# Record vectors of a recurrence block moved by DMA instead of turned on VectorE, in a decoder layer on Trainium2

## What is computed

```python
def step(S, inp):
    qt, kt, vt, at, gft = inp
    bs1 = jnp.einsum('bhk,bhkv->bhv', kt, S)
    S1 = S + at[..., :, None] * bs1[..., None, :]
    S2 = jnp.exp(gft)[..., None] * S1
    bs2 = jnp.einsum('bhk,bhkv->bhv', kt, S2)
    S3 = S2 + at[..., :, None] * bs2[..., None, :] + kt[..., :, None] * vt[..., None, :]
    o = jnp.einsum('bhk,bhkv->bhv', qt, S3)
    return (S3, o)
out = out3[:, -N:]   # out3 stacks z, z, o: only the last third of the steps' outputs are used
```

## Time and profile before

| | us |
|---|---|
| median of 3 runs | 2278.86 |
| lowest, highest | 2270.1, 2287.62 |
| the profiled execution | 2289.55 |
| its span | 2287.8 |
| DVE busy | 1961.8 (86%) |
| PE busy | 1758.8 (77%) |
| POOL busy | 1179.1 (52%) |
| ACT busy | 688.7 (30%) |

### The profile page before, as it was taken

How to read it: one execution, slowest core, us unless ns; L and a number is a source line. 1 busy time by engine, 2 the same in 40 slices (tenths; PEclk the granted TensorE clock), 3 DMA queues, 4 the chain that set the end, 5 groups by cost and what they waited for, 6 DMA issues and landing times.

```text
span 2287.8 us, 34138 instructions
## 1 busy us (share of the span) xinstructions
PE 1758.8 (77%) x10406; PEld 1336.9 (58%) x10406; DVE 1961.8 (86%) x5667; ACT 688.7 (30%) x1377; POOL 1179.1 (52%) x1477
## 2 busy tenths in 40 slices
PE   6278988998898889988998440268888799877993
PEld 3145767676667666776677320145675567755682
DVE  7999998999999999999899998999999999733000
ACT  3132244323432343234323100162223622243120
POOL 2445364564565545655575479474775665223103
PEclk8568998999999989998999765577998689977997
DMA  7111443354434444543355321110364133620353
GB/s 251 61 29 60 141 142 101 129 161 146 142 126 134 146 112 136 154 146 111 116 173 168 83 97 32 30 20 14 107 191 153 20 101 129 220 80 24 108 189 104
DMA packets 319121, 262.29 MB, mean 115 GB/s; under 512 B 157297, under 2 KB 292074, under 8 KB 318954
## 3 DMA queue, kind: packets, MB, share of 16 engines
q1 hardware_dynamic: 284874, 218.08, 30.8%
q10 hardware_dynamic: 27936, 25.44, 3.4%
q0 software_dynamic: 6144, 16.79, 2.3%
HBM read 217.82 MB, written 41.03 MB: 113 GB/s over the span
## 4 chain that ended last, share of the span: by engine, by line
PE 39%; DVE 33%; POOL 9%; ACT 7%; issue 6%; DMA 4%; SPq 2%; ACTq 0%; POOLq 0%; DVEq 0%; PEldq 0%
PE ps L740 9%; PE ps L731 8%; DVE ps L1750 7%; DVE ps L1731 6%; PE ps L676 5%; PE ps L667 5%; DVE prod L1723 5%; DVE terms L1738 4%; DVE terms L1733 3%; PE ps L613 2%; PE ps L600 2%; PE ps L624 1%; ACT hT L1054 1%; DMA pj<-in_wpT 1%; DVE rec_out L1672 1%
## 5 line engine op out<-in xcount | busy, mean ns | idle before, releaser
L1750 DVE TENSOR_REDUCE ps<-terms 128x64 f32<-128x320 f32 x1024 | 448.6, 483 | 0.0
L1731 DVE TENSOR_REDUCE ps<-prod 128x16 f32<-128x272 f32 x1024 | 397.2, 433 | 0.0
L1738 DVE TENSOR_TENSOR terms<-ps,rec_out 128x256 f32<-128x256 f32 x1024 | 381.8, 414 | 0.0
L731 PE MATMUL ps<-xg,fc 128*128 128x128 f32 x2848 | 356.5, 286 | 32.9 <-PE ps L740 11.5
L1723 DVE TENSOR_TENSOR prod<-ps,rec_in 128x256 f32<-128x256 f32 x1024 | 380.7, 413 | 0.1
L731 PEld LDWEIGHTS ps<-xg,fc 128*128 128x128 f32 x2848 | 346.1, 201 | 54.6 <-issue 46.9
L740 PE MATMUL ps<-pj,hT 128*128 128x256 f32 x1424 | 334.3, 388 | 32.8 <-ACT hT L1054 32.8
L740 PEld LDWEIGHTS ps<-pj,hT 128*128 128x128 f32 x1424 | 265.9, 192 | 85.7 <-ACT hT L1054 52.3
L667 PE MATMUL ps<-xtf,fc 128*128 128x512 f32 x512 | 244.6, 616 | 5.7 <-issue 3.4
L676 PE MATMUL ps<-pj,hT 128*128 128x256 f32 x1024 | 236.5, 382 | 0.0
L676 PEld LDWEIGHTS ps<-pj,hT 128*128 128x128 f32 x1024 | 195.1, 191 | 57.1 <-issue 34.4
(11 more groups left out here) (257 smaller groups left out, 3003.7 us busy)
## 6 DMA issues: line engine op xcount, KB each, us to landing
fc<-in_wfcT SPq DMA_DIRECT2D x80, 1024.0 KB, 5.1
pj<-in_wpT SPq DMA_DIRECT2D x80, 1024.0 KB, 7.9
xg_rows<-in_rows ACTq DMA_DIRECT2D x105, 128.0 KB, 2.1
rec_in<-early_rows SPq DMA_DIRECT2D x60, 192.0 KB, 2.8
out_rows<-y ACTq DMA_DIRECT2D x89, 128.0 KB, 5.7
early_rows<-vec SPq DMA_DIRECT2D x180, 32.0 KB
in_rows<-o_rows SPq DMA_DIRECT2D x2, 2176.0 KB, 17.5
out_rows<-o_rows SPq DMA_DIRECT2D x2, 2176.0 KB, 18.1
```

The lines of the kernel that those rows point to most:

```text
L731: i = mm(ps[:, UP + g // 4, g % 4 * P:(g % 4 + 1) * P], fc[:, par, c, g * P:(g + 1) * P], xg[:, c], start=c == 0, stop=c == KC - 1)
L1731: red(SE[:, old, cols, HD:EH].rearrange("p v n -> p n v"), prod[:, c % PLACED, :, cols, 0:HD + 1], AX.X, ALU.add).then_inc(step_done, 1)
L1738: tt(terms[:, cols, :, 0:NV], SE[:, old, cols, HD:EH].unsqueeze(2).to_broadcast([P, HC, HD, NV]), rec_out[:, c].unsqueeze(1).to_broadcast( ...
L1750: red(SE[:, new, cols, 0:HD], terms[:, cols, :, 0:NV + 1], AX.X, ALU.add).then_inc(step_done, 1)
```

## The change

- `vec` loses the slots of w and k. They move to `wk_rows`, with the four words of a vector element (two steps, w and k) side by side, so that one run of 64 words per chunk and head is what `rec_out` holds. `wk` is a view of it with a step of four words; ACT writes k into it (one more activation a step), POOL reads and writes it.
- From block 1 on, `lay_out` turns nothing but the queries of kept blocks. DVE waits for the end of POOL's list only in kept blocks. It waits for `early_in0` and `late_in0` ahead of a block's first chunk, and for `early_in1` and `late_in1` ahead of chunk 16's values.
- The values go with the early moves: 8 more DMAs to DRAM, each of 1,024 runs of 32 bytes, and one more read per half. They come first, behind `kv_sb` alone.
- `late_vectors` waits for operation 42 (47 for a kept block), writes w, k (4 DMAs, runs of 256 bytes) and the last input vector (4 DMAs, 64 bytes), waits for them to land and issues `late_records`, 4 reads per half. The list has the last product on `E_COL` ahead of those on z.
- `LAY` goes: POOL and ACT no longer wait for DVE's transposes of these vectors; ACT waits for `late_out`.
- POOL's list of a free block ends at chunk 27 instead of 32.
- In `FREE_AT` and `LATER_AT` steps are placed 1 to 5 later.

```diff
-LAY = CH + NV + 1
-LAY_KEPT = LAY + 2 * CH
+LAY_KEPT = 2 * CH
+LATE_READY, LATE_READY_KEPT = 42, 47
+        wk_rows = sb("wk_rows", [P, D, CH, 2])
+        wk = wk_rows[:, :, :, :].rearrange("p d i c -> p c i d")
...
             def early_vectors(sb_at):
+                sp.wait_ge(kv_sb, (sb_at + 1) * CH)
+                for b in range(B):
+                    rows = slice(b * NCH, (b + 1) * NCH)
+                    for i in range(CH):
+                        sp.dma_start(early_vals[rows].rearrange("g (n i v) -> n i g v", n=NCH, i=CH)[:, i],
+                                     vec[rows, i, V_COL].rearrange("n (g v) -> n g v", v=HV)).then_inc(early_out, 16)
                 sp.wait_ge(prep_pool, prep_before(sb_at) + EARLY_READY)
...
+            def late_vectors(sb_at):
+                if sb_at > 1:
+                    sp.wait_ge(late_in1, (sb_at - 1) * (LATE_READS * 16))
+                sp.wait_ge(prep_pool, prep_before(sb_at) + (LATE_READY_KEPT if sb_at >= KEEP else LATE_READY))
+                for b in range(B):
+                    rows = slice(b * NCH, (b + 1) * NCH)
+                    sp.dma_start(late_wk[b].rearrange("h (n x) -> n h x", n=NCH),
+                                 wk_rows[rows].rearrange("n d i c -> n (d i c)").rearrange("n (h x) -> n h x", h=H)).then_inc(late_out, 16)
+                    sp.dma_start(early_rows[EARLY, b].rearrange("h (n d) -> n h d", n=NCH),
+                                 vec[rows, 1, E_COL].rearrange("n (h d) -> n h d", h=H)).then_inc(late_out, 16)
+                sp.wait_ge(late_out, sb_at * (LATE_MOVES * 16))
+                late_records(sb_at, 0, late_in0)
...
+            def second_half(sb_at):
+                early_records(sb_at, 1, early_in1)
+                late_records(sb_at, 1, late_in1)
...
                 used(f, LATE + 1)
                 if m is not None:
                     early_vectors(first)
+                    late_vectors(first)
                 used(f, LATE + 2)
...
-                early_records(first, 1, early_in1)
+                second_half(first)
...
                 used(m, 0)
                 early_vectors(first + 1)
+                late_vectors(first + 1)
                 if f is not None:
                     store_tile(f)
                 for e in EXPERTS[1:3]:
                     used(m, e)
-                early_records(first + 1, 1, early_in1)
+                second_half(first + 1)
...
-                last = PREP_DONE_LATE if late else PREP_DONE_KEPT if keep else NCH
+                last = PREP_DONE_LATE if late else PREP_DONE_KEPT if keep else PREP_DONE
...
-                dve.wait_ge(prep_pool, prep_before(sb_at + 1))
-                for i in range(CH):
-                    nc.vector.transpose(vrec[:, :, i].rearrange("p n v -> p v n"), ...)
+                if sb_at == 0 or kept:
+                    dve.wait_ge(prep_pool, prep_before(sb_at + 1))
...
-                across(rec_in[:, NV - 1], by_d(vec[:, 1, E_COL]))
-                for i in range(CH):
-                    for kind in range(2):
-                        across(rec_out[:, :, :, 2 * i + kind], by_d(vec[:, i, (W_COL, K_COL)[kind]]))
...
+                if sb_at:
+                    dve.wait_ge(early_in0, sb_at * (EARLY_READS * 16))
+                    dve.wait_ge(late_in0, sb_at * (LATE_READS * 16))
                 place_v(0)
...
-FREE_AT = {1: 1, "caps": 46, "minima": (40, 42, 43, 44), "divided": 61, "resid": 66, 2: 66, "routing": 85, "places": 93, "rows": 94, "gather": 82, "scatter": 95, "combine": 101, 3: 112}
+FREE_AT = {1: 1, "caps": 46, "minima": (41, 43, 44, 45), "divided": 64, "resid": 70, 2: 70, "routing": 90, "places": 98, "rows": 99, "gather": 84, "scatter": 100, "combine": 103, 3: 114}
```

More of the change, by code:

```diff
@@ L73 @@
 PREP_FROM, PREP_FROM_KEPT, PREP_FROM_SECOND, PREP_DONE_KEPT = 13, 5, 4, 29
-PREP_FROM_LATE, PREP_DONE_LATE = 10, 31
+PREP_FROM_LATE, PREP_DONE_LATE, PREP_DONE = 10, 31, 27
 LAY_FIRST = CH + 2 * NV + 1
-LAY = CH + NV + 1
-LAY_KEPT = LAY + 2 * CH
-KC_SLOTS = W_COL, K_COL, V_COL, XK_COL, E_COL = range(5)
+LAY_KEPT = 2 * CH
+W_COL, K_COL = range(2)
+V_COL, XK_COL, E_COL = range(3)
 EARLY = NV
 EARLY_READY = 26
-EARLY_MOVES = EARLY * B
+VALUE_MOVES = CH * B
+EARLY_MOVES = EARLY * B + VALUE_MOVES
+EARLY_READS = 5
+LATE_READY, LATE_READY_KEPT = 42, 47
+LATE_MOVES = 2 * B
+LATE_READS = 4
 HALF = NCH // 2
@@ L348, in early_records @@
                 chunks = slice(half * HALF, (half + 1) * HALF)
+                sp.dma_start(vrec[:, chunks].rearrange("g n i v -> g (n i v)"),
+                             early_vals[:, half * (HALF * CH * HV):(half + 1) * (HALF * CH * HV)]).then_inc(done, 16)
                 for dst, kind in ((rec_in[:, 0:EARLY - 1, chunks], slice(0, EARLY - 1)), (rec_g[:, chunks].unsqueeze(1), slice(EARLY - 1, EARLY))):
@@ L352, in early_records, with late_records @@
                         sp.dma_start(dst[v:P:2].rearrange("q c n d -> q c (n d)"), src).then_inc(done, 16)
+            def late_vectors(sb_at):
[10 more added lines that the diff above has]
+                late_records(sb_at, 0, late_in0)
+            def late_records(sb_at, half, done):
+                sp.wait_ge(step_done, (sb_at - 1) * (NCH * STEP) + 2 + (half + 1) * (HALF * STEP))
+                chunks = slice(half * HALF, (half + 1) * HALF)
+                for dst, src in ((rec_out[:, chunks].rearrange("q n d k -> q (n d k)"), late_wk.rearrange("b h n -> (b h) n")),
+                                 (rec_in[:, NV - 1, chunks].rearrange("q n d -> q (n d)"), early_rows[EARLY].rearrange("b h n -> (b h) n"))):
+                    n = src.shape[1] // 2
+                    for v in range(2):
+                        sp.dma_start(dst[v:P:2], src[:, half * n:(half + 1) * n]).then_inc(done, 16)
+            def second_half(sb_at):
+                early_records(sb_at, 1, early_in1)
+                late_records(sb_at, 1, late_in1)
             def store_tile(m):
@@ L1653, in first_preparation @@
                 then(tt(heads(e), heads(zp[:, :]), by_head(hsum[:, 3]), ALU.mult))
-                for kind, col in enumerate((K_COL, E_COL)):
+                for kind, col in enumerate((wk[:, K_COL, 1], vec[:, 1, E_COL])):
                     after()
-                    then(tt(zp[:, :], z, by_step(vec[:, 1, col]), ALU.mult))
+                    then(tt(zp[:, :], z, by_step(col), ALU.mult))
                     sums(dots[:, kind])
```

66 lines of the change are left out of this document (37 added, 29 removed).

## The result

The changed kernel takes 2374.7 us (median of 4, 2366.45 to 2382.3), the kernel before 2275.71 in the same comparison (2270.1 to 2287.62): ratio 1.0414, 95% interval 1.038 to 1.0448. It is 4.1% slower. I had predicted 2248, and the result lies above my whole range.

The account below looks back on a forecast made before the run. VectorE was taken as the bound, PE next. Terms summed to -31.2 us, taken as -31: 2289.55 profiled to 2258.5, or 2248 against the 2278.86 median; own range 2237 to 2257, 8 in 10: 2222 to 2283.

Parts of the forecast that it names:

- 19.6 us of waits that PE would get back: In periods 1 to 4: 15.6 us for shifted scores, 1.5 for `chosen`, 2.5 for an expert's weights.
- DVE bounds, PE some 8 us behind: In period 2 VectorE is busy 223.7 of 224.9 us; with its load gone PE is the next bound.
- PE gets back the scores' wait, -15.6: In periods 1 to 4, earlier minima on VectorE end PE's wait for shifted scores: 4 x 3.9 us.
- Rival 2: PE gives nothing back, as the scores' wait is a chain only partly VectorE's: 2263 us, chance 0.18.
- the two smaller waits: PE's waits in period 2 for `chosen` (1.46 us) and an expert's weights (2.46 us), both counted as regained.
- Late rows priced at 0: At boundaries in periods 1 to 4, VectorE's waiting for PE covers the late rows; bound 2 us at each of five boundaries.
- Value moves at 0.53 us each: In the SP queue, each of 8 more DMAs per block takes 0.53 us to issue, hidden behind the wait for GpSimd.
- Rival 4: Value moves of 32-byte runs drain slowly, 8 taking 17 us instead of 4: about +60 us, 2308, chance 0.12.
- POOL's strides at 0: GpSimd's operations on keys and w 4 words apart cost nothing extra, judged from 32-element tree additions.
- Rival 3: GpSimd slows by its strides, half as much again on some 15 operations per block: +28 to +31, about 2278, chance 0.12.
- Later steps, +1.8 and -7.5: Five steps' later routing starts period 0 1.8 us late; behind tile 4's routing, five steps fewer gain 7.5 us.
- From tile 4's routing to the end, -18.8: VectorE leads again: -7.5 for fewer steps, -5.7, -5.7 and -3.1 at boundaries, +3.2 for the output store behind five reads.

Follow-up runs that it names:

- b2_list27: The kernel before with only GpSimd's list in a free block ended at chunk 27 instead of 32: ratio 0.9966.
- d2_strides: The changed kernel with all rows turned by VectorE and steps at the old places, leaving interleaved rows and the list to chunk 27: 1.0115, 2305.8 us.
- d1_all_dve: As d2_strides, but with the steps at the later places of the changed kernel: 1.0259, 2342.8 us.
- a4_values_dve: The changed kernel with the values turned by VectorE again and no value moves or reads by DMA: 1.0216, 2333.9 us.
- a1_divided: The changed kernel with "divided" at step 62, ahead of the block boundary, instead of 64: 1.0271, 2350.6 us.
- a3_values_apart: The changed kernel with the eight value moves issued one load earlier in the SP queue: 1.0248, 2341.1 us.
- d4_filler7: d1_all_dve with 7 idle matmuls of 128 rows ahead of PE's wait for "divided": 1.0169, 2318.1 us.
- c2_mix: The changed kernel with values turned by VectorE, second weights load ahead of late rows, "divided" at 62 and list to chunk 30: 1.0091, 2302.7 us.

## Why the prediction was wrong

Set one behind the other, the runs make a ledger from the kernel before to the changed one. Each ratio is known to 0.3 or 0.5%, so the first line to 7 us, and each other one, a difference of two ratios, to some 15.

| added | runs compared | us |
|---|---|---|
| list to chunk 27 | b2_list27, before | -8 |
| w and k four words apart (with one more activation a step and the list's new order) | d2_strides, b2_list27 | +34 |
| steps placed later | d1_all_dve, d2_strides | +33 |
| w, k, last row by DMA | a4_values_dve, d1_all_dve | -10 |
| values by DMA | changed kernel, a4_values_dve | +45 |
| together | | +94 |

The steps that failed are terms of the sum: 0 for the value moves, 0 for the strides, nothing for the first preparation, and later steps as a gain of 5.7 us on balance. Above all the sum counted 19.6 us of waits that PE would get back. By the steps of the prediction:

- **DVE bounds, PE some 8 us behind.** Right as far as it was tested: filling PE's stop on b2_list27 gave nothing, and DVE's busy time fell by 65 us. How far behind PE is, no run measures by itself.
- **PE gets back the scores' wait, -15.6.** Wrong. It is 3.88 us in periods 1 to 4 of every run in which no filler stands ahead of it. Rival 2 had the number, but not the reason, and nor had I: neither DVE nor POOL is in this wait. Here it is in period 2, before and then after (ACT, and POOL's shift of the same scores):

```profile
571.20 2.25 POOL L1234 TENSOR_TENSOR probs<-probs,least 128x1232 f32<-128x1232 f32 x1 [3.49 <-DVE least L1484]
574.33 0.39 ACT L1060 ACTIVATE y<-ps 128x256 f32<-128x256 f32 x1 [3.62 <-PE ps L740]
575.42 1.28 ACT L964 ACT_TABLE_LOAD   x1 [0.70 <-ACT y L1060]
576.71 2.36 ACT L964 ACTIVATE probs<-probs 128x1232 f32<-128x1232 f32 x2
...
600.29 4.46 POOL L1289 TENSOR_TENSOR probs<-probs,least 128x1232 f32<-128x1232 f32 x2
602.50 0.38 ACT L1115 ACTIVATE y<-ps 128x256 f32<-128x256 f32 x1 [3.62 <-PE ps L793]
603.59 1.28 ACT L1019 ACT_TABLE_LOAD   x1 [0.70 <-ACT y L1115]
604.88 2.35 ACT L1019 ACTIVATE probs<-probs 128x1232 f32<-128x1232 f32 x2
```

  Before, the first shift is done at 573.45, ahead of ACT. What ACT does is copy out PE's own last pass, load a table and take the first exponential, 3.88 us from PE's last matmul whatever the others do. Even the later shift of the changed kernel (two in the row, the first done near 602.5) is there in time. No earlier DVE could have given this back. With 64 us of DVE work taken off (a4_values_dve against d1_all_dve), the gain is 10 us, not told from none. Of the two smaller waits the 1.46 us for `chosen` did go in period 2; the 2.46 for weights became 7.5 to 8.3 at the ends of periods 1 to 3.
- **Late rows priced at 0.** Wrong. I let DVE's wait for PE at "resid", step 70, cover the rows' way. But rows are wanted at the boundary, step 64, and behind it, ahead of "resid", stands "divided", which PE waits for. DVE may have time left at step 70; PE has lost its own by then. What I called a bound of 0 to 2 us is 4.4 to 11.4 us at 10 boundaries, 71.4 in all. With the values turned by DVE it is 17.0 in all and 4.7 at most, so the greater part comes with the value moves. With "divided" ahead of the boundary DVE's waits for rows are as long (70.3 us against 71.4), and 33 us come back (a1_divided).
- **Value moves at 0.53 us each.** Wrong by 2.6 times. The row I took them from had no load just ahead. I had even seen the queue push back (3.31 us for three) and used it only for a rival. And the kernel before has the row that was wanted, the 16 moves at 1262 us right behind a load:

```profile
1261.57 0.47 SPq L315 DMA_DIRECT2D pj<-in_wpT  x1
1262.14 4.48 SPq L340 DMA_DIRECT2D early_rows<-vec  x3
...
1275.95 0.49 SPq L340 DMA_DIRECT2D early_rows<-fbuf  x1
```

  They take 14.3 us, where I took 8.4. Rival 4 comes nearest: it put +60 us, and the values cost 45. From release to rows it is 38 us, where it decides at 45 and I counted 31; the issues take 11.1 us, where it had 17. I gave it 0.12. Its reason, runs of 32 bytes, was at most half right. The same 8 moves of 32-byte runs, all 15 blocks of a3_values_apart and of the changed kernel taken: 10.6 to 13.7 us when they begin within 2 us of a load's issue (18 times), 8.3 or 8.4 when 4 us behind it, 4.6 to 8.1 when 10 us or more. So the time of an issue goes by the place in the queue. It is not all of the 38 us: in a3_values_apart the moves of 6 blocks still take 10.6 to 12.1 us right behind a load, but ahead of PE's release, where less waits for them. The 7 us left of the 45 are not told from none. The Trainium skill (DMA: Bandwidth & Descriptors, "Specifications"), which the prediction set beside this rival, asks for runs of 512 bytes; no run here moved these values in runs that long.
- **POOL's strides at 0.** Wrong. The tree rows of 32 elements were far from the 512-element operations. The Trainium skill (GPSIMD Engine Reference, "Performance pitfalls for Q7 kernels") speaks of about half as much again per element for such steps. Here it was 19 to 23% on most of the 512-element forms, 3 us a block, so its direction holds and its size doesn't. Rival 3 named the output sums and kept blocks: in d2_strides period 5 is 3.1 us longer and period 6 2.8, against b2_list27. The free periods are 12 longer and the start 5, and what follows period 6 is 10 shorter. That is 14 us between the two profiled executions; the medians are 34 apart by ratio, and no trace shows where the other 20 lie.
- **First preparation not priced at all.** DVE computes it on the same rows. Its 512-element operations take 1.05 to 1.10 us where they took 0.69, thirteen of them, which is the 5 us by which all steps start later.
- **Later steps, +1.8 and -7.5.** Mis-sized: +12 on the kernel before, +33 with rows that come late or slowly. The missing term is the clock. I counted a stop of PE at its own length; behind it PE runs at 0.50 for up to 16 us, and filling the stops gave back 21 of the 33 us, known to some 13 (d4_filler7).
- **From tile 4's routing to the end, -18.8.** None of the gain came: periods 5 and 6 are within 2 us of the kernel before, and what follows is 8 us longer. For the store, put at +3.2, DVE's wait for `o_rows` in period 7 went from 3.4 to 17.8 us. It is 15.7 without the value moves, 4.5 in d2_strides and 2.8 in d1_all_dve, so most of it comes with the late moves and reads in SP's queue. The mechanism was right and more than 4 times larger.

**What stays open.** How the 34 us of the layout split beyond the 5 us of the start; a kernel with the words packed for POOL and interleaved only for the moves was not tried. Nor is it settled what DVE's wait for capped scores (44.5 us) costs. In period 2 of the changed kernel it is 12.6 us and stands ahead of the boundary, where DVE then waits 8.9 us more for rows: they go out when PE's release and the queue let them, so there it did not set the time of the boundary. In c2_mix the wait is 4.9 us in all, in d1_all_dve 8.6 in period 1 and 1.3 to 2.0 in periods 2 to 4. No run shows why the queue takes longer over a move right behind a load, nor why 24 matmuls of one row did not hold the clock that 7 of 128 rows held: they differ in number as well as in rows.

The lowest ratio is that of b2_list27, 0.34% under the kernel before: the one part of the change that may be worth keeping alone, by an interval that just excludes none.

## What to carry to other kernels

Price a DMA issue from a row that has the same neighbours in its queue, here a load of 2 MB just ahead, and not from one of the same kind. Look through the whole trace for such a row; here there was one. Before calling a wait covered by a later stop of the same engine, check what stands between the two that another engine waits for. Before counting on a wait to go, find what starts its last step: PE's 3.88 us began at PE's own last matmul, and no earlier work elsewhere could shorten them. A stop of PE costs its length plus what the lower clock takes behind it, so that one small step moved by two places was worth 33 us here.

## What the hardware showed that I had not expected

- Eight DMAs of 1,024 runs of 32 bytes each take 1.3 to 1.7 us apiece to issue right behind a load of 2 MB, and mostly 0.6 to 0.7 from 10 us behind it on.
- VectorE's products of 512 float32 elements took 1.06 us with elements 16 bytes apart, 0.69 packed; GpSimd's 1.55 and 1.28.
- A stop of 3.5 us on TensorE was followed by 16 us at half clock, and 7 idle matmuls in the stop's place made the program 21 us faster. Twenty-four of one row, in the same place, were themselves slowed after 2.7 us: their records came 0.43 us apart instead of 0.21.
- ScalarE's way from PE's last matmul to the first exponential (a copy of 0.39 us, a table load of 1.28, an exponential of 1.2 and the hand-overs) made PE wait 3.88 us in each free period of every kernel without a filler there.
